# Other places for the stages between the attentions of a two-layer decoder on one core

## The reference, cut to what matters

```
x = layernorm(x + splat_attention(x))                  # 16 heads of 16, softmax of Gaussian weights
x = layernorm(x + cross_attention(x, ctx))             # 16 heads of 16, 120 keys
x = layernorm(x + gate * (x @ expert_w[argmax] + b))   # 8 experts, the best one, all 8 are computed
x = layernorm(x + causal_attention(x))                 # 16 heads of 16
x = layernorm(x + block(x, ctx))                       # self (32 wide, masked after the softmax) and cross attention,
                                                       # each followed by gelu(ln(x) @ li2 + b) @ li3 + b, 256 -> 1024 -> 256
x = layernorm(x + sum over the top 4 of 16 experts of relu(x @ keys[e]) @ values[e] * gate)
```

## Time and profile before

| | us |
|---|---|
| median of 3 runs | 4038.72 (4036.19 to 4040.62) |
| the profiled execution | 4046.9, span of its instructions 4045.1 |
| PE busy | 3320.6 (82%) |
| PEld busy | 2479.6 (61%) |
| DVE busy | 2804.8 (69%) |
| ACT busy | 2097.5 (52%) |
| POOL busy | 976.5 (24%) |
| mean granted clock of TensorE | 0.802 |

### The profile page before, as it was taken

How to read it: one execution, slowest core, us unless ns; L and a number is a source line. 1 busy time by engine, 2 the same in 40 slices (tenths; PEclk the granted TensorE clock), 3 DMA queues, 4 the chain that set the end, 5 groups by cost and what they waited for, 6 DMA issues and landing times. The chain is left out here.

```text
span 4045.1 us, 92628 instructions
## 1 busy us (share of the span) xinstructions
PE 3320.6 (82%) x37680; PEld 2479.6 (61%) x37680; DVE 2804.8 (69%) x6362; ACT 2097.5 (52%) x4222; POOL 976.5 (24%) x1808
## 2 busy tenths in 40 slices
PE   2988887888888888988888888888887888888876
PEld 1666565666665666656656656666655676666654
DVE  5767675777676766766777667677776676767655
ACT  4645555455456554554564554545555555455552
POOL 0212332122232321131132222212332112124310
PEclk9778787887797878867968888787877896977887
DMA  5000000000000000000000000000000000000000
GB/s 159 2 3 2 1 2 5 6 10 3 2 2 2 7 3 7 7 3 2 7 2 2 5 4 7 5 4 2 2 2 3 9 9 3 2 2 2 2 4 6
DMA packets 30357, 31.36 MB, mean 8 GB/s; under 512 B 8673, under 2 KB 26482, under 8 KB 29938
## 3 DMA queue, kind: packets, MB, share of 16 engines
q1 hardware_dynamic: 29938, 25.44, 2.0%
HBM read 21.24 MB, written 4.19 MB: 6 GB/s over the span
## 5 line engine op out<-in xcount | busy, mean ns | idle before, releaser
L1101 ACT ACTIVATE p<-bank,p_log 128x512 f32<-128x512 f32 (+2 forms) x1280 | 746.6, 583 | 1334.9 <-PE bank L795 1261.9
L1667 POOL TENSOR_TENSOR prob<-p,prob 120x256 f16<-120x256 f32 (+2 forms) x512 | 458.9, 896 | 1790.0 <-ACT prob L1102 1789.7
L1102 ACT ACTIVATE prob<-bank,p_log 128x512 f16<-128x512 f32 (+2 forms) x1280 | 747.5, 584 | 0.0
L1366 DVE TENSOR_REDUCE negm<-bank 128x2 f16<-128x512 f32 (+1 forms) x1280 | 675.1, 569 | 12.7 <-PE bank L750 3.2
L772 PE MATMUL bank<-q,k 32*128 32x256 f16 (+2 forms) x6144 | 567.8, 319 | 95.7 <-issue 37.4
L1284 DVE TENSOR_TENSOR prob<-p,prob 128x512 f16<-128x512 f32 (+2 forms) x768 | 467.7, 616 | 234.0 <-ACT prob L1102 224.2
L772 PEld LDWEIGHTS bank<-q,k 32*128 32x128 f16 (+1 forms) x6144 | 345.6, 121 | 211.6 <-issue 95.1
L795 PE MATMUL bank<-ident_h,negm 128*128 128x256 f16 (+2 forms) x2560 | 439.4, 301 | 0.0
L1676 POOL TENSOR_SCALAR_AFFINE_SELECT probm<-prob 128x128 f16<-128x128 f16 x1024 | 323.9, 355 | 346.8 <-DVE prob L1284 346.8
L750 PE MATMUL bank<-k,q 32*128 32x256 f16 (+2 forms) x2560 | 252.8, 282 | 156.4 <-DVE negm L1366 144.0
L840 PEld LDWEIGHTS bank<-v,prob 128*128 128x128 f16 (+1 forms) x8448 | 334.5, 103 | 75.7 <-DVE prob L1284 37.1
(11 more groups left out here) (298 smaller groups left out, 6393.4 us busy)
## 6 DMA issues: line engine op xcount, KB each, us to landing
x<-in_x SPq DMA_DIRECT2D x16, 256.0 KB, 2.7
out<-z SPq DMA_DIRECT2D x16, 256.0 KB, 2.2
xa<-in_li SPq DMA_DIRECT2D x9, 256.0 KB, 4.5
x<-in_li SPq DMA_DIRECT2D x7, 256.0 KB, 5.0
z<-in_wq SPq DMA_DIRECT2D x4, 256.0 KB, 4.3
z<-in_li SPq DMA_DIRECT2D x4, 256.0 KB, 5.3
cx<-in_ctx_t SPq DMA_DIRECT2D x16, 60.0 KB, 1.8
cx<-in_ctx SPq DMA_DIRECT2D x16, 60.0 KB, 1.8
```

The costliest lines, as they stand in the source:

```text
L1101: act(p32[0:n, g % PBUF32, 0:cols], ps[0:n, 0:cols], ACT.Exp, bias=p_log[0:n, :], scale=a.scale)
L1102: act(prob[0:n, 0, g % PBUF, 0:cols], ps[0:n, 0:cols], ACT.Exp, bias=p_log[0:n, :], scale=a.scale).then_inc(a_done, one(a_done))
L1366: v.tensor_reduce(negm[:, h * NT:(h + 1) * NT], ring_v[bank_of(e, v_full)][:, :].rearrange("p (t n) -> p t n", t=NT)[:, :, 0:ATTNS[k].keys ...
L1667: g.tensor_tensor(prob[0:n, 1, m % PBUF, 0:cols], p32[0:n, m % PBUF32, 0:cols], prob[0:n, 0, m % PBUF, 0:cols], ALU.subtract).then_inc(pp_ ...
```

## The change

The change moves stages to other turns and cuts some in two:

- `LANE_ORDER` is written out as a list of 80 lanes in place of a repeated period of 13.
- The experts of chain 2 stood in stages "best" (expert 0), "experts" (1 to 3) and "experts2" (4 to 7). Now expert 0 stays in "best" and experts 1 to 7 have "e1" to "e7", each a turn; "e8" is the end of the norm.
- Each hidden layer's second stage, "h1" or "r1", held the second half of the features' product and the first half of the product behind it. The latter (and for "r1" the gates' mix) is now "h1b" or "r1b". On VectorE the addition of the first half and the split of the second move to "h1b" with it; "h1" holds nothing there.
- Every chain has its own LATE places (LATE_OTHER is gone), and most places in EARLY, LATE and LATE_SOON differ.
- The number that a low part's semaphore has is taken from a list, LOW_NUMBER, made once; the numbers are the same.

```
-PERIOD = (0, 1, 0, 2, 1, 0, 2, 0, 1, 2, 0, 1, 2)
-LANE_ORDER = (1, 2) + PERIOD * 6
+LANE_ORDER = (
+    0, 1, 0, 2, 1, 2, 0, 1, 2, 0, 1, 2, 0, 1, 2, 0,
+    1, 0, 1, 2, 0, 2, 0, 1, 2, 0, 1, 2, 0, 1, 0, 2,
+    1, 0, 2, 0, 1, 2, 0, 1, 2, 0, 1, 0, 2, 1, 0, 2,
+    0, 1, 2, 0, 1, 2, 0, 1, 0, 2, 1, 0, 2, 0, 1, 2,
+    0, 1, 2, 0, 1, 0, 2, 1, 0, 2, 1, 0, 2, 1, 0, 2,
+)
...
 EARLY = {
     0: (),
-    1: (("oT", 9), ("out", 11), ("out2", 12)),
-    2: (("oT", 9), ("out", 11), ("out2", 12), ("xT_e", 15), ("router", 17), ("best", 21), ("experts", 23), ("experts2", 27), ("experts3", 30)),
-    3: (("oT", 9), ("out", 12), ("norm2", 15), ("norm3", 17), ("norm4", 20)),
-    4: (("oT", 9), ("out", 11), ("out2", 12), ("ctx", 16), ("ctx2", 17), ("xoT", 18), ("h0", 22), ("h1", 23), ("h2", 26), ("norm3", 28), ("norm4", 29)),
-    TAIL: (("oT", 9), ("out", 11), ("out2", 12), ("xoT", 16), ("h0", 18), ("h1", 21), ("h2", 25), ("h3", 26), ("xT", 29), ("sel", 31)),
+    1: (("oT", 10), ("out", 12), ("out2", 14)),
+    2: (("oT", 9), ("out", 11), ("out2", 12), ("xT_e", 14), ("router", 17), ("best", 20), ("e1", 21), ("e2", 22), ("e3", 23), ("e4", 24), ("e5", 25), ("e6", 26), ("e7", 27), ("e8", 31)),
+    3: (("oT", 9), ("out", 12), ("norm2", 15), ("norm3", 18), ("norm4", 20)),
+    4: (("oT", 9), ("out", 11), ("out2", 12), ("ctx", 13), ("ctx2", 14), ("xoT", 15), ("h0", 17), ("h1", 19), ("h1b", 23), ("h2", 26), ("norm3", 31), ("norm4", 32)),
+    TAIL: (("oT", 9), ("out", 11), ("out2", 12), ("xoT", 15), ("h0", 17), ("h1", 19), ("h1b", 20), ("h2", 23), ("h3", 24), ("xT", 27), ("sel", 29)),
 }
 LATE = {
-    0: (("xT", 2), ("q_raw", 4), ("q", 7), ("k_raw", 10), ("k", 15), ("v", 18)),
-    TAIL: (("gates", 2), ("r0", 4), ("r1", 8), ("r2", 10), ("r3", 11)),
+    0: (("xT", 2), ("q_raw", 3), ("q", 5), ("k_raw", 11), ("k", 13), ("v", 18)),
+    1: (("xT", 3), ("q", 11), ("k", 14), ("v", 28)),
+    2: (("xT", 1), ("q", 8), ("k", 10), ("v", 18)),
+    3: (("xT", 10), ("q", 13), ("k", 17), ("v", 21)),
+    4: (("xT", 4), ("q", 11), ("k", 13), ("v", 17)),
+    TAIL: (("gates", 2), ("r0", 4), ("r1", 6), ("r1b", 8), ("r2", 10), ("r3", 11)),
 }
-LATE_OTHER = (("xT", 2), ("q", 10), ("k", 13), ("v", 19))
-LATE_SOON = {1: (("xT", 16), ("q", 21), ("k", 27), ("v", 29)), 3: (("xT", 24), ("q", 26), ("k", 31), ("v", 33))}
+LATE_SOON = {1: (("xT", 17), ("q", 22), ("k", 26), ("v", 28)), 3: (("xT", 22), ("q", 26), ("k", 29), ("v", 30))}
...
                         if part == 1:
+                            yield
                             token_major(w2, 0, DM, hidT, 4, token_tiles, "v", bias=bias,
...
                         for n in range(EXPERTS):
-                            if n in (1, 4):
+                            if n > 0:
                                 yield
```

More of the change, by code:

```diff
@@ L148, in low_on_pool, with low_numbers @@
     return g % PAIR == 1 and not ATTNS[ORDER[g][0]].keep_after
+def low_numbers():
+    made = {False: 0, True: 0}
+    for g in range(len(ORDER)):
+        made[low_on_pool(g)] += 1
+        yield made[low_on_pool(g)]
+LOW_NUMBER = list(low_numbers())
 def ends_group(a, h):
@@ L186, in places @@
     last = PHASE[k, b] - 1 if k < TAIL else first + 1
-    late = LATE_SOON[k] if k > 0 and last == first else LATE.get(k, LATE_OTHER)
+    late = LATE_SOON[k] if k > 0 and last == first else LATE[k]
     for stage, at in late:
@@ L601, in low_made_of @@
             def low_made_of(g):
-                on_pool = low_on_pool(g)
-                return pp_ready if on_pool else ps_ready, sum(low_on_pool(m) == on_pool for m in range(g + 1))
+                return pp_ready if low_on_pool(g) else ps_ready, LOW_NUMBER[g]
             def loads_of(b):
@@ L1151, in between_attentions @@
                             ACT.Copy).then_inc(a_done, one(a_done))
-                        yield
-                        yield
-                        yield
+                        for n in range(EXPERTS):
+                            yield
                     if k >= 4:
@@ L1697, in between_attentions @@
                     if k == 2:
-                        for step in ("xT_e", "router", "best", "experts"):
+                        for step in ("xT_e", "router", "best", "e1", "e2", "e3", "e4", "e5", "e6"):
                             yield
@@ L1705, in between_attentions @@
                     if k >= 4:
-                        for step in ("xoT", "h0", "h1"):
+                        for step in ("xoT", "h0", "h1", "h1b"):
                             yield
@@ L1713, in between_attentions @@
                     if k == 5:
-                        for step in ("xT", "sel", "gates", "r0", "r1"):
+                        for step in ("xT", "sel", "gates", "r0", "r1", "r1b"):
                             yield
```

2 lines of the change are left out of this document (1 added, 1 removed).

## The result

The changed kernel took 4055.05 us in the median (4051.95 to 4057.30, six runs) against 4038.18 us (4034.90 to 4045.34, six runs) for the kernel before: a ratio of 1.0039, 95% interval 1.0026 to 1.0052. It is slower by about 16 us where 50 us less were forecast. The time lies inside the stated range of 3895 to 4080 us, but the forecast had the wrong sign.

A forecast was written before the change was run, and what follows sets the result against it. TensorE, busy 82% of the span at a mean clock share of 0.802, was taken to set the pace, though not alone. Waits -16 us and clock -34 us gave -50 us, from 4038.7 to 3989 us; range 3895 to 4080 us.

The forecast's parts named there:

- the clock: TensorE's clock: dense stages packed in layers 4 and 5 and fewer long stalls shorten low-clock time; -34 us, bounds -75 to +40.
- (1): Lane order written out: only the start and neighbours near the end change; cost nothing, bounds -10 to +10 us.
- (2): Layer 4's "norm3" from turn 28 to 31: shorter waits for masked probabilities; -26 us, bounds -45 to 0.
- (3): Layer 3's "xT" from turn 2 to 10 at longer gaps, half its stall hidden; -16 us, bounds -33 to +5.
- (4): "sel" from turn 31 to 29, "gates" staying at 34: waits for transposed gates drop to about 6 us; -11 us.
- (5): One turn per expert and per hidden-layer half frees VectorE: -5 us each, bounds -20 to +10 and -25 to +10.
- (6): "xT_e", "best" and layer 5's "xoT" each one turn nearer the stage before: more waiting, +22 us, bounds +10 to +35.
- (7): Layer 4's "xoT" from 18 to 15, context norm earlier: normalisation beside GpSimd's addition adds waits; +25 us, bounds 0 to +60.
- Rival D: Slower: layer 4's "xoT" stalls exceed 2 us in the mean and the clock falls; +55 us, middle 4065, chance 0.28.
- (8): Layer 5's "h2", "h3", "xT" keep their spacing, leaving the largest repeated stall unchanged; 0, bounds -10 to +15 us.
- signs named ahead: Right: masked-probability waits well under 42 us, gates under 10, clock above 0.81. Wrong: normalised-tile transpose waits well above 99.1 us.
- Rival C: Waits moved, not removed: they reappear one slot on; 4035 us, chance 0.12.

The follow-up runs named there:

- a_tail: Changed kernel with layer 5 at its old turns; ratio 1.0039 to the kernel before.
- a_exp: Changed kernel with chain 2's old early places (experts in three turns, "xT_e" 15, "best" 21, "e8" 30); ratio 0.9992 to the kernel before.
- a_late2: Changed kernel with layer 2's old late list ("xT" 2, "q" 10, "k" 13, "v" 19); ratio 0.9983 to the kernel before.
- a_c4: Changed kernel with layer 4 at its old turns, its norms staying at 31 and 32; ratio 1.0040 to the kernel before.
- a_two45: Changed kernel with chain 2's old early and late places and layers 4 and 5 at their old turns, norms staying new; ratio 0.9906 to the kernel before.
- a_two: Changed kernel with chain 2's old early places (experts in blocks) and old late list; ratio 0.9944 to the kernel before.
- a_lane: Changed kernel with the old order of turns (LANE_ORDER as repeated period of 13); ratio 1.0114 to the kernel before.
- b_best2: Kernel before with new order of turns, layer 3's new late list, layer 4's norms at 31 and 32 and its new late list; ratio 0.9864, 3977.8 us.
- b_late3: Kernel before with only layer 3's new late list ("xT" 10, "q" 13, "k" 17, "v" 21); ratio 0.9917.

## Why the prediction was wrong, step by step

Between the forecast of -50 us and the measured +16 lie 66 us. Four terms were too good: the clock (-34 forecast, but the time at 1.2 GHz stayed at 1597 us for 1602), the experts' turns (-5 forecast, a cost of some 19), layer 2's late list (no term, a cost of some 23) and the norm of layer 4 (-26 forecast, -3 alone). Three gains were larger than priced: the order of turns, layer 3's late list, and the lists for a gap of one phase, which had no term and are worth 18 us in the changed kernel. The steps one by one:

(1) *Order of turns, 0 ± 10:* -12 us alone, -30 us in the changed kernel. The forecast priced the few phases that differ at one wait each; the start and the end of the run weren't read for their own waits. Alone, the gain is in TensorE's busy time and not in its waits; why stays open.

(2) *norm3 at 31, -26:* -3 us alone. The row read was right (42.1 to 24.0 us for masked probabilities), the sum wasn't: it asked for the cover of the row maxima, not for that of "xT" at turn 34, which the norm feeds. And with that mended only another 5 us came, as the row maxima's wait rose instead: the step took a wait in a row for time on the path.

(3) *Layer 3's "xT" at 10, -16:* -34 us alone, -26 in the changed kernel. The mechanism stands, and so does its size for the waits: TensorE's idle time fell by 18 us. What the term left out is the clock, with 23 us less of busy time.

(4) *Gates, -11:* didn't happen, the wait rose from 17.1 to 37.4 us. By stage, layer 5's "gates" went from 17.2 to 21.1 us, so two turns more before it brought nothing; a_tail, with "sel" at 31 again and all of layer 5 as before, has 17.1. The other 18.2 us lie at chain 2's "best", now at 20, where 14.4 us of the earlier trace rows were put down to "v" before. No run took this step alone.

(5) *A turn for each expert, -5, and for each half of a layer, -5:* after the clock, this step failed most. VectorE's 126.9 us fell to 73.7, as said, and nothing shows that it was worth anything on the path. The experts' list costs 0.47% (a_exp), about 19 us, in a band that ended at +10. The prediction looked at the last expert and the norm; what it missed is the expert at the first turn of a slot ("e4"), whose product waits for the addition of the expert before, 13.9 us in 16 places. That the old blocks have no such wait is shown; what the rest of the 19 us is isn't.

(6) *Tightened pairs, +22:* waits of this size came (32.3 to 56.5 us ahead of "xT_e" and "xT"), mostly from another cause. Layer 5's "xoT" is as priced: at 16 again in a_tail it waits 9 us less (39.8 to 30.4), for 7 in the sum. The pair at "xT_e" wasn't too tight; "k" of layer 2's late list at 10 stood ahead of the other chain's sum. That list, 23 us by a_late2, has no term in the prediction at all. Without it the changed kernel is 0.17% faster than the kernel before, not 0.39% slower.

(7) *Layer 4's "xoT" at 15, +25:* the stalls came as priced, 29.0 us in 16 chains, 1.8 us each, 2.59 us in the one shown. But TensorE's idle time in all is less with them than without, so they can't be added to the time; what the packing costs is busy time. Rival D put its threshold at stalls of over 2 us in the mean, and they are shorter. Its fall of the clock ahead of "h0" is there, only smaller: by stage, TensorE is busy 8 us longer for the same products of layer 4's "h0" when packed (57.8 us for 49.4 in a_c4, 61.1 for 52.8 in a_two45), where D had 56.

(8) *Layer 5's "xT", 0:* right, 55.9 to 55.1 us.

*Clock, -34:* the largest miss, and for the packing its sign is wrong. With layers 4 and 5 packed the low time is 67 us longer (a_two against a_two45); at the 12% to 35% of the earlier trace rows that is 8 to 23 us, and 15 were measured. In a_c4 and a_tail the clock rose too (0.808), and their ratios didn't move, so the price per microsecond isn't confirmed by this one pair. The 35% isn't a bound either: it compares the durations of matmuls that overlap. The starts of the products of the earlier trace rows lie 213 ns apart at 0.50 and 109 ns apart at 1.00, so that a stretch that TensorE fills with them costs 49% of its low time. What failed is the belief that dense stages closer together would shorten the low time; the slots behind them lost what the dense ones had won, in the phase shown.

Of the signs named ahead, masked-probability waits came out "right" (20.2 us). The waits for the gates (37.4 us for under 10) and the clock (0.803 for above 0.81) did not, and the transposes' waits came out "wrong", well above 99.1 us.

The steps of the chain above are -12, -32, +7, -2, +15 and +38 us. They add up to the 16 us by construction, each being the difference of two neighbours, so their sum says nothing for the account. Rival C had the mechanism that the waits show, moved and not removed. The outcome is on D's side, by parts that neither named, so D isn't confirmed by it.

## What to carry to other kernels

When engines work through fixed queues, price a moved step at both ends: who stands behind it at the new place, on every queue, and what it feeds, and go through every changed place this way, the ones that look harmless too. A wait that falls in the profile is a gain only if nothing else waits in its stead: sum the idle time of the pacing engine, not the rows, and set its busy time beside it, since the clock can take back what the waits gave. Undo parts together as well as singly, since the sum of single runs can be off; the parts of a change are worth separating, as two of these alone made the kernel 1.1% faster.

## What the runs showed of the hardware

Mean clock and time went together in most runs: from 0.799 (a_lane, 4078 us) over 0.803 (after, 4052 us) to 0.818 (b_best2, 3975 us) for the same 37680 matmuls. Not in all: a_two has 0.801 and 4013 us, a_c4 and a_tail 0.808 and 4044 and 4045 us. Executions of one kernel differ in the same way: on one chip the kernel before took 4027.57 us at 0.810 and 4044.23 us at 0.802, so busy times of single profiles hold to some 10 us (an estimate from this spread). Between before and b_late3 TensorE's busy time fell by 22.8 us and its low time by 81 us (1602 to 1521), which is 28% of the low time, within the 12% and 35% of the earlier trace rows. Unexpected was that packing dense stages lowered the clock (0.809 to 0.801); the windows above show the low stretch behind the packed stages, but every edit of places changes stalls and density at once, so the cause stays open.

The normalisation beside GpSimd's addition took 2.01 us in layer 4 as in the earlier trace rows (1.07 us in the "xT_e" lines above, without it), so the price was to be had from the rows of the kernel before. A table load of ScalarE took 1283 ns each time, and two stages of one function in one slot shared it (95 loads before, 65 after).
